# Graph network on one core: node update of layer 0 spread over two iterations, and landing waits for GpSimd in layer 1

## What is computed

```python
h = relu(layernorm(x))                                  # layer 0
agg = segment_sum(h[src], dst)
x = x + (agg @ W_rel.T + b_rel + h @ W_root.T)
h = relu(layernorm(x))                                  # layer 1
m = h[src] * (silu(edge_attr @ We1 + be1) @ We2 + be2)
agg = segment_sum(m, dst)
x = x + h + silu(agg @ Wn1 + bn1) @ Wn2 + bn2
```

## Time and profile before

| | us |
|---|---|
| median of 3 runs | 4783.59 |
| the runs | 4771.58, 4783.59, 4814.32 |
| the profiled execution | 4752.23 |
| its span in the profile | 4750.4 |
| layer 0's loop, about | 250 to 2290 |
| layer 1's loop, about | 2340 to 4740 |

### The profile page before, as it was taken

One profiled execution on the slowest core, in us unless ns is written; L12 is line 12 of the kernel. 1 busy time (PEld: TensorE's weight loads), 2 busy tenths in 40 slices (PEclk: granted clock), 3 DMA queues, 4 the chain that ended last, 5 costly groups with the idle time before them and its releaser, 6 DMA issues.

```text
span 4750.4 us, 29563 instructions
## 1 busy us (share of the span) xinstructions
PE 2158.6 (45%) x7600; PEld 1272.9 (27%) x7600; DVE 2216.7 (47%) x2541; ACT 739.0 (16%) x1263; POOL 2999.1 (63%) x3135
## 2 busy tenths in 40 slices
PE   1112111111111111111347777777777777778778
PEld 0111001010101101011124444444444444444444
DVE  5889577575875759567612222222222222222222
ACT  2400000000000000000112222222222222222222
POOL 6376757577575776757366666666666666666663
PEclk9975555555555555555567778777778777778788
DMA  4212212122221222212122222222222222222222
GB/s 118 80 52 59 59 47 64 46 59 58 53 60 46 62 53 56 59 45 66 49 60 65 65 67 66 65 68 66 64 65 66 66 64 69 67 65 66 65 64 63
DMA packets 230578, 296.56 MB, mean 62 GB/s; under 512 B 68964, under 2 KB 160278, under 8 KB 230433
## 3 DMA queue, kind: packets, MB, share of 16 engines
q0 software_dynamic: 100096, 205.20, 16.7%
q10 hardware_dynamic: 61378, 60.59, 4.7%
q1 hardware_dynamic: 69086, 30.60, 2.4%
HBM read 269.68 MB, written 26.48 MB: 62 GB/s over the span
## 4 chain that ended last, share of the span: by engine, by line
DVE 31%; another core or an unknown queue 24%; PE 24%; issue 16%; ACT 2%; DVEq 2%; POOL 0%; DMA 0%; ACTq 0%; SPq 0%; POOLq 0%
DVE wide L894 14%; PE wide L459 7%; PE wide L454 6%; PE seg L415 6%; DVE xs L900 4%; DVE onehot L900 3%; DVE ys L900 3%; PE ew_b L465 2%; PE ew_a L465 2%; DVE onehot L883 1%; DVEq L911 1%; DVE onehot L865 1%; DVE agg L907 1%; PE node L473 1%
## 5 line engine op out<-in xcount | busy, mean ns | idle before, releaser
L353 POOL DMA_INDIRECT rows<-h_rows,idx x3060 | 2926.7, 956 | 1666.4 <-issue 1023.2
L894 DVE TENSOR_TENSOR wide<-rows,consts_ps 128x1536 f32<-128x1536 f32 (+1 forms) x414 | 691.7, 1671 | 44.1 <-issue 32.6
L415 PE MATMUL seg<-onehot,rows 128*128 128x128 f32 x3128 | 538.4, 329 | 372.7 <-DVE agg L924 281.3
L1051 DVE TENSOR_TENSOR rows<-ew_a,rows 128x512 f32<-128x512 f32 x207 | 142.8, 690 | 1104.2 <-remote 508.7
L459 PE MATMUL wide<-hidden,we_sb 128*128 128x512 f32 x784 | 549.1, 789 | 191.4 <-ACT hidden L647 187.9
L415 PEld LDWEIGHTS seg<-onehot,rows 128*128 128x128 f32 x3128 | 491.9, 240 | 411.5 <-DVE agg L924 310.2
L647 ACT ACTIVATE hidden<-wide,be_col 128x512 f32<-128x512 f32 x393 | 270.0, 687 | 1555.0 <-remote 934.8
L1051 DVE TENSOR_TENSOR rows<-ew_b,rows 128x512 f32<-128x512 f32 x184 | 126.7, 689 | 565.8 <-PE ew_b L465 190.2
L405 PE MATMUL seg<-onehot 128*128 128x128 f32 x138 | 37.8, 447 | 667.3 <-DVE agg L907 477.4
L652 ACT ACTIVATE agg<-wide,be_col 128x512 f32<-128x512 f32 x392 | 268.3, 684 | 293.9 <-PE wide L459 146.0
L454 PE MATMUL wide<-ef_a,we_sb 50*128 50x512 f32 x418 | 274.9, 743 | 29.5 <-DMA ef_a<-ef_blocks 25.6
(11 more groups left out here) (174 smaller groups left out, 1688.5 us busy)
## 6 DMA issues: line engine op xcount, KB each, us to landing
rows<-h_rows,idx POOLq DMA_INDIRECT x3060
ef_a<-ef_blocks ACTq DMA_DIRECT2D x70, 300.0 KB
node_work<-ef_blocks ACTq DMA_DIRECT2D x47, 300.0 KB
xs<-x SPq DMA_DIRECT2D x40, 256.0 KB
ys<-y_rows SPq DMA_DIRECT2D x26, 256.0 KB
out<-xs ACTq DMA_DIRECT2D x26, 256.0 KB
y_rows<-ys ACTq DMA_DIRECT2D x25, 256.0 KB
h_rows<-node_work ACTq DMA_DIRECT2D x23, 256.0 KB
```

The costliest lines, as they stand in the source:

```text
L353: pool.indirect_dma_start(out=rows[:, u, t, :], out_offset=None, in_=table, in_offset=bass.IndirectOffsetOnAxis(ap=idx[:, j:j + 1], axis=0 ...
L415: mm = pe.matmul(seg_ps[:, 0:P], rows[:, u, t, :], onehot[:, g % 2, k * TB + t, :], start=(k == 0 and t == 0), stop=(last and t == TB - 1))
L894: v.tensor_tensor(picked[:, 0:tiles, :], rows[:, first:first + tiles // TB, :, :].rearrange("p k t f -> p (k t) f"), run_mask[:, r, first ...
L1051: v.tensor_tensor(rows[:, u, :, :], ew, rows[:, u, :, :], ALU.mult).then_inc(s_msg, 1)
```

## The change

In layer 0 the node update of one iteration is spread over that iteration and the next. TensorE does the product ahead of group 4 (before: 3) and turns it back ahead of group 1 of the next iteration. ScalarE does the rest of the earlier update around `turned` of this one; the biased product goes to a buffer of its own for set 0 (`node_work[:, 0, :]`) so that `aggT` is free. VectorE does x1 of the earlier update at group 2, its shift at group 3 and y at group 4. The first and the last update stand outside the loops. SyncE's loop has `next_idx` ahead of `node_x`. In layer 1 GpSimd gets two further waits per iteration: ahead of group 3 for the landing of its own group 2, and behind group 5 for the landing of that one (`STOPS`); in layer 0 the list is empty.

```diff
+STOPS = ([], [3, 6])
...
+        biased = [node_work[:, 0, :], *aggT[1:]]
...
                 with sp.Fori(1, ITERS) as it:
+                    next_idx(0, p * ITERS + it, it)
                     node_x([loop_group(it)], p * (ITERS - 1) + it - 1)
-                    next_idx(0, p * ITERS + it, it)
...
+                    if g in STOPS[layer]:
+                        hold(pool, s_rows[layer][g - 1], landed(i, g - 1))
                     if layer == 0:
                         hold(pool, s_pick[R - 1], i * G + (g + 1))
...
+                if G in STOPS[layer]:
+                    hold(pool, s_rows[layer][G - 1], landed(i, G - 1))
...
-                        tr = pe.transpose(node_o[r][:, t * D:(t + 1) * D], aggT[r][:, t * P:(t + 1) * P], ident[:, :])
+                        tr = pe.transpose(node_o[r][:, t * D:(t + 1) * D], biased[r][:, t * P:(t + 1) * P], ident[:, :])
...
-                with pe.Fori(1, ITERS) as it:
-                    i = p * ITERS + it
-                    steps = node_update0(p * (ITERS - 1) + it - 1, 0)
+
+                def edges0(it, first):
+                    n = p * (ITERS - 1) + it - 1
                     for g in range(G):
-                        if g in steps:
-                            steps[g]()
-                        run_sums(i, g)
+                        if g == 1 and not first:
+                            node_update0(n - 1, 0)[4]()
+                        if g == 4:
+                            node_update0(n, 0)[3]()
+                        run_sums(p * ITERS + it, g)
+
+                edges0(1, True)
+                with pe.Fori(2, ITERS) as it:
+                    edges0(it, False)
+                node_update0((p + 1) * (ITERS - 1) - 1, 0)[4]()
...
-                    nc.scalar.activation(aggT[r], node_t[r][:, :], ACT.Identity, bias=b_rel_col[:, :]).then_inc(s_nbias, 1)
+                    nc.scalar.activation(biased[r], node_t[r][:, :], ACT.Identity, bias=b_rel_col[:, :]).then_inc(s_nbias, 1)
...
-                with act.Fori(1, ITERS) as it:
+
+                def node_steps(it):
                     n = p * (ITERS - 1) + it - 1
-                    side_by_side([node_update0(loop_group(it), n, 0, (p * ITERS + it) * G + LAG, n + 1)])
+                    return node_update0(loop_group(it), n, 0, (p * ITERS + it) * G + LAG, n + 1)
+
+                node_steps(1)[0]()
+                with act.Fori(2, ITERS) as it:
+                    steps, earlier = node_steps(it), node_steps(it - 1)
+                    earlier[1]()
+                    earlier[2]()
+                    steps[0]()
+                    earlier[3]()
+                    earlier[4]()
+                    earlier[5]()
+                last = node_steps(ITERS - 1)
+                for k in (1, 2, 3, 4, 5):
+                    last[k]()
...
                 steps = node_update0(n, 0, n + 1)
+                steps[3]()
                 steps[4]()
                 steps[5]()
...
-                    if g == 0 and not first:
+                    if g == 2 and not first:
+                        earlier[3]()
+                    if g == 3 and not first:
                         earlier[4]()
-                    if g == 1 and not first:
+                    if g == 4 and not first:
                         earlier[5]()
-                    if g == G - 1:
-                        steps[3]()
```

More of the change, by code:

```diff
@@ L979, in edges0 @@
                 landed_last = dve.snap(landed(i, G - 1))
-                steps, earlier = node_update0(n, 0, n + 1), node_update0(n - 1, 0, n)
+                earlier = node_update0(n - 1, 0, n)
                 for g in range(G):
```

## The result

The changed kernel takes 4869.3 us (median of 4 runs, 4864.8 to 4871.6), the kernel before on that occasion 4787.3 us (4 runs, 4771.6 to 4814.3): a ratio of 1.0158 with a 95% interval of 1.0128 to 1.0189, or 75 us (61 to 90); the two medians lie 82 us apart. The prediction had 4823 us with the range 4715 to 4870, that is +40 us. The direction came out, and the size was half of what came.

The account below looks back on a forecast made before the run. TensorE's late signals beside gathers were taken to bound layer 0, with GpSimd's stops paying. Terms +33 + 0 + 3 + 4 = +40 us on the 4783.6 us median gave 4823 us, range 4715 to 4870.

Parts of the forecast that it names:

- SyncE's order: Layer 0, index load ahead of the node load: shorter, more frequent GpSimd stops let less of TensorE's word through, +33 us.
- the spread: Layer 0, node update moved across groups and iterations: waits shift within VectorE's idle time, 0 on GpSimd (-40 to +20).
- the +20: Layer 0, upper end of the node update's allowance: adds stalling at an iteration's start, just ahead of the pick, +20 us.
- Rival E: Layer 0: x1 asks for a turning back as few groups old as before, VectorE stalls as now; 4791 us, chance 0.06.
- That is the bound of layer 0: Layer 0: TensorE's late word falls some 30 us behind per iteration until GpSimd must stop, costing 225 us.
- a fixed 119 us per iteration: Layer 0: time TensorE's signals need beside gathers, 6 x 16.1 + 2 x 11 us, against 85 us of gathers.
- The end of layer 0, +3 us: Last update of layer 0: x1, its statistics and ScalarE's two steps now stand behind the last group, +3 us (0 to +10).
- Layer 1, +4 us: Two landing stops per iteration in layer 1: mostly hidden beside GpSimd's waits for TensorE's sum, +4 us (bounds -46 to +101).
- rival D: Layer 1: landing stops add in full, +101 us, total 4920 us, chance 0.06; its mark was layer 1 growing over 20 us.
- A: Layer 0: debt decides, GpSimd stops every third iteration for the pick as long as for the index; 4791 us, chance 0.20.
- B: Layer 0: the index chain was the price, stops of 7 us meet the debt; 4728 us, in full 4665, chance 0.20.
- C: Layer 0, group 0 after a partial stop: every second iteration stops for longer; 4849 to 4893 us, chance 0.16.

Follow-up runs that it names:

- f4: Changed kernel with VectorE's x1, shift and y each one group later (3, 4, 5), layer-1 stops kept; late chip, 1.0023 of the kernel before.
- e4: Changed kernel without the two layer-1 landing stops; late chip, 4886.1 us, 1.0089 of the kernel before.
- e1: Kernel before with one edit, next_idx ahead of node_x in SyncE's layer-0 loop; late chip, 4821.4 us for 4843.4 us, 0.9949.
- e2: Changed kernel with SyncE's old order put back, node_x ahead of next_idx; late chip, 1.0013 of the kernel before.
- f2: Changed kernel with TensorE multiplying one of three rounds of each group's sums in layer 0; late chip, one execution, 4768 us for 4818.
- e3: Kernel before with only the two landing stops per iteration in layer 1; late chip, 0.9989 of the kernel before.

## Why the prediction was wrong

The sum's sign came out by luck. Its one large term, +33 for SyncE's order, measured the other way, and the term that does cost, the spread, stood in it with 0.

- **SyncE's order.** Right: no stop is released by the index, the picks release them, and there are more of them. Wrong: the price. The +33 us were put on shorter, more frequent stops (one of 20 and one of 28.3 in four iterations, 48.3 us). The order alone gave one stop of 22 us in two iterations and a gain of 0.5% on one late chip; on a prompt chip nothing. This step of the sum should have been about -22, not +33. Nor is it so that the index load "waits only for landed rows": it stands behind the `node_x` of the iteration before in SyncE's queue, and so behind y. The last bytes of the first half arrive 16 to 32 us before GpSimd needs them in the changed kernel, not 45, and where y is a group later (f4) they come too late. The 10.5 us for "two index DMAs" are the stretch between two issues with a wait for rows between them; no term hangs on it.
- **The spread, "on GpSimd I allow 0".** This is the step that failed. I had named the +20 ("adds that stall just ahead of the pick") and taken 0, because "VectorE has 2040 - 1460 us idle". Measured alone (e4 against e1) the spread costs 65 us. VectorE's idle time is no cover: it is waiting for TensorE's word, none of it for rows, and so it is part of the chain that sets the pace. GpSimd follows VectorE's picks group by group, and x1's wait of 19 to 26 us at group 2 lands on the pick of group 3. Moving x1 one group on gave back 42 us of layer 0 at the start of layer 1. The rest of the 65, among it what the new places of TensorE's and ScalarE's steps do, wasn't taken apart. Rival E had the fact right (x1 asks for a word as fresh as before) and drew "the rhythm stays" from it.
- **"That is the bound of layer 0".** The late word sets the pace, but not as a fixed 119 us per iteration: e2 makes all sums and products in 97.9 us, and VectorE doesn't wait for TensorE once in the steady part. And with a third of the sums the stops vanish and the iteration still takes 95.2 us (f2). So of the 225 us of stops and stretch that I read as the word's price, little could have been won: if f2's 95.2 us is the floor of the others too, the cycles stand 0.7 us per iteration above it before (95.9) and 3.8 after (297 / 3 = 99.0).
- **The end of layer 0, +3 us.** It was 31 in the last iteration, whose stops I had no term for, and 15 behind it (30 and 11 on the second late chip, e4 against e1): VectorE is further behind when the last gather ends, and x1, shift and y of the last update come on top. No run separates the two.
- **Layer 1, +4 us.** Right on the late chip where the stops ran alone: -5 us (interval -14 to +3) of 4843. In the first pair of profiles layer 1 grew by 22.5 us, which passes the prediction's own mark for D (20 us), and no run shows how much of that is the change. On prompt chips it is rival D and beyond its bound: I had 2.2 us for each of 46, +101; the stop at the end of an iteration is 4.4 us beyond the gap in the row shown, and 154 to 161 us came between the first gather of layer 1 and the end. Why it costs twice the 2.1 us at group 3 isn't shown; the prediction's word on the loop's branch, which stands behind that wait, was only argued. The Trainium skill's 2.0 us per DMA (DMA: Bandwidth & Descriptors, Anatomy of one DMA — SWDGE (gpsimd) path) would have given 46 x 2.0 = 92 us as an estimate; the stop ahead of group 3, 2.37 us with its restart, is near it, the other one is twice that.
- **The other rivals.** A (the rhythm stays) and B (stops of 7 us alone) were ruled out by 19 and more stops by the pick and a longer cycle; C, more and longer stops, was the nearest in size (4849 to 4893 us), but its place was wrong: group 0, where the stops came ahead of groups 2 and 3.
- **The rule that an increment costs 26 ns** (the Trainium skill, TensorE: Matmul & The Clock Gate, The cost: per-tile semaphore tail): by it rival B would have come out. On a prompt chip the trace agrees with the rule (0.03 us from the product to the bias), on a late chip it doesn't (27 us in the earlier trace rows, 53 in the next iteration). And where it holds, B still gives nothing, since no index load is ever late there.

Open: why the first profile of before has 95.9 us per iteration and e3, with the same layer-0 code on another late chip, 98.7; how far the first pair's 22 us in layer 1 are the change; why the first pair differs by 75 us where the parts measured on the second late chip give -22, +65 and -5; and what makes a chip late.

## What to carry to other kernels

An engine with idle time is still no cover for a wait if another engine follows it step by step: place a wait whose length can't be shortened where the next thing behind it is needed last, and in small pieces. A saving has to be measured against the floor of the resource that it feeds, and the floor is found by taking the suspected work out, as with the two thirds of the sums here. A stop that costs nothing because others stand in the same place costs its full length where they don't, so it pays to see more than one chip. And before idle time is booked as room to spare, ask what it waits for: if it never waits for its supplier, the engine is the one that sets the pace.

## What the hardware showed that I had not expected

- The same program took 4054 to 4063 us on three chips and 4787 to 4843 on three others, 18% to 19.5% more. On the late ones TensorE's word comes late beside gathers, in the kernel before up to 53 us: its product ends at 1113.1 and ScalarE's bias, which waits for nothing else, starts at 1165.9 (timeline of ScalarE below). In f2 a long row of gathers slowed from 1.25 to 1.40 us each. On the prompt ones neither shows.

```profile
1165.89 0.69 ACT L591 ACTIVATE node_work<-node,b_rel_col 128x512 f32<-128x512 f32 x1 [57.23 <-remote]
```

- While it lasts, the delay holds for TensorE's signals in order, some 16 us per group of six matmuls and six weight loads; asking one group later shortens the wait by one such piece (26.5 to 10.9 us).
- A stop of GpSimd lets the word catch up: with 13 us of silence in each iteration of 97.9 us (e2) VectorE waits for TensorE nowhere in the steady part.
- The version that beats both kernels on a late chip and equals the kernel before on a prompt one is the smallest: the kernel before with SyncE's two lines exchanged, 0.9949 (0.9932 to 0.9965) and 0.9999.
